# First cross-attention: context loaded first, the first LayerNorm ahead of masks, biases and the values' projection

## The reference, cut to what matters

```python
def _layernorm(x, axis=-1, eps=1e-05):
    m = jnp.mean(x, axis=axis, keepdims=True)
    v = jnp.var(x, axis=axis, keepdims=True)
    return (x - m) / jnp.sqrt(v + eps)

def _L0_xattn_ref(q, k, v, Wq, bq, Wk, bk, Wv, bv, Wo, bo):   # 16 heads of 8
    qh, kh, vh = proj(q, Wq, bq), proj(k, Wk, bk), proj(v, Wv, bv)
    scores = jnp.einsum('bhqd,bhkd->bhqk', qh, kh) / np.sqrt(hd)
    scores = jnp.where(jnp.triu(jnp.ones((S, S), bool)), NEG, scores)
    attn = jax.nn.softmax(scores, axis=-2)
    ...                                            # mixed with vh, then Wo and bo
```

## Time and profile before

| | |
|---|---|
| median of three runs | 3425.03 us |
| the profiled execution's own time | 3413.21 us |
| its span | 3411.4 us |
| TensorE's granted clock, mean | 0.982 of full speed |
| busy, share of the span | PE 95%, DVE 86%, POOL 77%, ACT 70% |
| first matmul of the scores | 20.7 us |
| last step of the first block's pipeline with scores | about 221 us |
| first matmul of the local layers | 244.9 us |

### The profile page before, as it was taken

How to read it: one execution, slowest core, us unless ns; L and a number is a source line. 1 busy time by engine, 2 the same in 40 slices (tenths; PEclk the granted TensorE clock), 3 DMA queues, 4 the chain that set the end, 5 groups by cost and what they waited for, 6 DMA issues and landing times.

```text
span 3411.4 us, 130897 instructions
## 1 busy us (share of the span) xinstructions
PE 3245.9 (95%) x56355; PEld 2054.7 (60%) x56386; DVE 2943.4 (86%) x3343; ACT 2379.1 (70%) x4288; POOL 2639.8 (77%) x1408
## 2 busy tenths in 40 slices
PE   7977999999999999999999999999999999977996
PEld 4545666666666666666666666666666666643554
DVE  6869989889999999998989898898999999935887
ACT  6865677667676767676776776776767676746885
POOL 1229988888888888888888888888888888833576
PEclk9989999999999999999999999999999999988998
DMA  2002333443433344334433334343344333330000
GB/s 94 2 1 64 122 113 111 120 126 114 120 112 112 117 126 119 113 108 126 125 113 117 112 110 123 119 120 113 113 125 125 118 111 112 110 123 1 2 11 17
DMA packets 229188, 336.05 MB, mean 99 GB/s; under 512 B 39046, under 2 KB 151044, under 8 KB 228228
## 3 DMA queue, kind: packets, MB, share of 16 engines
q1 hardware_dynamic: 228612, 327.68, 31.7%
HBM read 124.14 MB, written 102.76 MB: 67 GB/s over the span
## 4 chain that ended last, share of the span: by engine, by line
PE 84%; issue 5%; POOL 4%; ACT 3%; DVE 3%; SPq 0%; DMA 0%; POOLq 0%; DVEq 0%; ACTq 0%
PE psum L732 29%; PE psum L800 10%; PE psum L742 9%; PE psum L786 8%; PE psum L759 8%; PE psum L827 7%; PE psum L838 4%; POOL f_rotated L1154 2%; ACT x_expo L1480 1%; PE psum L817 1%; PE psum L809 1%; ACT x_expo L391 1%; PE psum L1337 1%; PE psum L1347 1%; PE psum L309 1%
## 5 line engine op out<-in xcount | busy, mean ns | idle before, releaser
L732 PE MATMUL psum<-w_qkv,f_xs 128*128 128x512 f32 x2304 | 1081.2, 606 | 18.9 <-issue 14.2
L1154 POOL TENSOR_TENSOR f_rotated<-f_times_cos,f_times_sin 128x1024 f32<-128x1024 f32 x384 | 908.7, 2367 | 9.3 <-DVE f_times_sin L1027 9.3
L1162 POOL TENSOR_TENSOR f_rotated<-f_rotated,f_rnorm 128x1024 f32<-128x1024 f32 x384 | 722.6, 1903 | 38.2 <-ACT f_rnorm L907 11.9
L732 PEld LDWEIGHTS psum<-w_qkv,f_xs 128*128 128x128 f32 x2304 | 410.1, 191 | 402.4 <-issue 393.6
L896 ACT ACTIVATE f_squares<-psum 128x1024 f32<-128x1024 f32 x384 | 392.9, 1023 | 361.4 <-PE psum L732 356.4
L1146 POOL TENSOR_TENSOR f_probs<-f_probs,f_rowsum 128x1024 f32<-128x1024 f32 x192 | 365.2, 1902 | 329.1 <-DVE f_rowsum L1066 329.1
L1026 DVE TENSOR_TENSOR f_times_cos<-psum,rot 128x1024 f32<-128x1024 f32 x384 | 469.8, 1223 | 131.6 <-ACT f_squares L896 127.8
L914 ACT COPY f_qkT<-psum 128x1024 f32<-128x1024 f32 x384 | 369.9, 1013 | 210.8 <-PE psum L742 210.7
L1027 DVE TENSOR_TENSOR f_times_sin<-psum,rot 128x1024 f32<-128x1024 f32 x384 | 466.1, 1214 | 0.0
L1034 DVE TENSOR_REDUCE f_sumsq<-f_squares 128x16 f32<-128x1024 f32 x384 | 463.4, 1209 | 0.0
L742 PEld LDWEIGHTS psum<-consts,f_rotated 128*128 128x128 f32 x3072 | 348.5, 141 | 98.0 <-issue 89.2
(11 more groups left out here) (175 smaller groups left out, 5159.5 us busy)
## 6 DMA issues: line engine op xcount, KB each, us to landing
f_v_moved<-f_v SPq DMA_DIRECT2D x768, 128.0 KB, 2.8
turned_blocks<-w_qkv SPq DMA_DIRECT2D x192, 512.0 KB, 3.0
f_probsT<-turned_blocks SPq DMA_DIRECT2D x768, 128.0 KB, 2.8
w_qkv<-in_l_wqkv SPq DMA_DIRECT2D x18, 512.0 KB, 4.0
w_o<-in_l_wo SPq DMA_DIRECT2D x6, 512.0 KB, 4.6
w_qkv<-in_ctxT SPq DMA_DIRECT2D x1, 2048.0 KB, 8.7
out<-x_f_result SPq DMA_DIRECT2D x8, 256.0 KB, 2.2
w<-in_l_w SPq DMA_DIRECT2D x6, 341.0 KB
```

The costliest lines, as they stand in the source:

```text
L732: mm = pe.matmul(pairs[i][:, j * BANK:(j + 1) * BANK], xs[g % 2][:, u % GB, :], w_qkv[:, part * INNER + j * BANK:part * INNER + (j + 1) * ...
L1154: pool.tensor_tensor(rotated[u % 2][:, part].rearrange("p h (s d) -> p s h d", s=2), halves(times_cos[part][:, :]), halves(times_sin[part] ...
L1162: pool.tensor_tensor(rt, rt, rnorm[u % 2][:, part * H:(part + 1) * H].unsqueeze(2).broadcast_to([P, H, HD]), ALU.mult).then_inc(normalised ...
```

## The change

Four edits. The context's first load is issued ahead of weights and tables; the tables (`consts`) are issued last of these. DVE no longer casts the masks and makes the biases before its first `centre`, but after it, in a function `constants()` called in step -5. ACT waits for the biases in step -3 rather than before its first square. And the lag of `variance_0` goes from -3 to -4, for all eight groups.

```diff
@@ first_attention @@
             MEAN, CENTRE, SQUARE, VARIANCE, ROOT, SCALE = (
-                {"0": -6, "f": 7}, {"0": -6, "f": 7}, {"0": -5, "f": 7}, {"0": -3, "f": 8}, {"0": -3, "f": 8}, {"0": -2, "f": 9})
+                {"0": -6, "f": 7}, {"0": -6, "f": 7}, {"0": -5, "f": 7}, {"0": -4, "f": 8}, {"0": -3, "f": 8}, {"0": -2, "f": 9})
...
             def sp(sp):
-                for dst, src in ((w_k, "wkT"), (b_k, "bk"), (w_v, "wvT"), (w_q, "wqT"), (b_q, "bq"), (w_o, "woT")):
-                    sp.dma_start(dst[:, :], dram[f"x0_{src}"]).then_inc(loaded, 16)
-                sp.dma_start(b_o[:, :], dram["x0_bo"]).then_inc(loaded, 16)
-                sp.dma_start(b_v[:, :], dram["x0_bv"].partition_broadcast(P)).then_inc(loaded, 16)
...
                 sp.dma_start(ctx2[:, first], dram["ctxT"][:, first]).then_inc(ctx_loaded, 16)
+                for dst, src in ((w_v, "wvT"), (w_k, "wkT"), (b_k, "bk"), (w_q, "wqT"), (b_q, "bq"), (w_o, "woT"), (b_o, "bo")):
+                    sp.dma_start(dst[:, :], dram[f"x0_{src}"]).then_inc(loaded, 16)
+                sp.dma_start(b_v[:, :], dram["x0_bv"].partition_broadcast(P)).then_inc(loaded, 16)
+                sp.dma_start(consts[:, :], dram["consts"]).then_inc(consts_loaded, 16)
                 sp.dma_start(x2[:, rest], dram["xT"][:, rest]).then_inc(rest_loaded, 16)
...
             def act(act):
                 act.preload_act_table_set("natural_log_exp_and_others")
-                act.wait_ge(biases_made, BIASES)
                 act.wait_ge(eps_made, 1)
...
                 for step in range(FIRST, LAST):
+                    if step == FIRST + 3:
+                        act.wait_ge(biases_made, BIASES)
...
             def dve(dve):
-                dve.wait_ge(loaded, LOADED)
-                dve.wait_ge(gates_ready, 1)
-                dve.tensor_scalar(b_q[:, :], b_q[:, :], inv_root, None, ALU.mult).then_inc(biases_made, 1)
...
+                def constants():
+                    dve.wait_ge(consts_loaded, 16)
+                    dve.tensor_copy(ident_bf[:, :], ident).then_inc(masks_ready, 1)
...
+                    dve.wait_ge(loaded, LOADED)
+                    dve.wait_ge(gates_ready, 1)
...
                 for step in range(FIRST, LAST):
+                    if step == FIRST + 1:
+                        constants()
```

More of the change, by code:

```diff
@@ L432, in dve @@
             def dve(dve):
-                dve.wait_ge(loaded, LOADED)
-                dve.wait_ge(gates_ready, 1)
-                dve.tensor_scalar(b_q[:, :], b_q[:, :], inv_root, None, ALU.mult).then_inc(biases_made, 1)
-                dve.tensor_scalar(b_k_part[:, :], head_parts, b_k[:, 0:1], None, ALU.mult).then_inc(biases_made, 1)
-                dve.tensor_tensor(gated_b_o[:, :], b_o[:, :], gates[:, 0:1], ALU.mult).then_inc(biases_made, 1)
-                dve.wait_ge(biases_made, BIASES)
+                def constants():
+                    dve.wait_ge(consts_loaded, 16)
+                    dve.tensor_copy(ident_bf[:, :], ident).then_inc(masks_ready, 1)
+                    for g in range(GB):
+                        dve.tensor_copy(mask_past[:, g, :], consts[:, P + NEAR:2 * P + NEAR]).then_inc(masks_ready, 1)
+                    dve.wait_ge(loaded, LOADED)
+                    dve.wait_ge(gates_ready, 1)
+                    dve.tensor_scalar(b_q[:, :], b_q[:, :], inv_root, None, ALU.mult).then_inc(biases_made, 1)
+                    dve.tensor_scalar(b_k_part[:, :], head_parts, b_k[:, 0:1], None, ALU.mult).then_inc(biases_made, 1)
+                    dve.tensor_tensor(gated_b_o[:, :], b_o[:, :], gates[:, 0:1], ALU.mult).then_inc(biases_made, 1)
+                    dve.wait_ge(biases_made, BIASES)
                 dve.wait_ge(x_loaded, 16)
@@ L1777, in _ @@
             sp.dma_start(xres[:, 0:GB * REST, :].rearrange("p b s -> p (b s)"), dram["xT"][:, 0:REST * GT]).then_inc(x_loaded, 16)
-            sp.dma_start(consts[:, :], dram["consts"]).then_inc(consts_loaded, 16)
             sp.dma_start(gates[:, 0:2], dram["g_xattn"].partition_broadcast(P)).then_inc(gates_loaded, 16)
@@ L1803, in _ @@
         def _(dve):
[L1804 to L1807, removed]
             x0_dve(dve)
```

## The result

The changed kernel takes 3443.16 us (median of six runs, 3437.63 to 3452.78), where the kernel before took 3424.65 on the same chip: a ratio of 1.0058, with a 95% interval of 1.0041 to 1.0075, which is 14 to 26 us slower. The forecast was 3445. The profiled execution is the longest of the six (3452.78 us), so its terms may come out larger than the median.

What follows compares the result with a forecast made beforehand. In the first block a DVE-ACT loop sets three steps of four, PE's chain the fourth. Start -2.8, bank wait +18.4 and clock +4.8 give +20.4 us: 3445.4 on a median of 3425.0, range 3437 to 3458.

Steps and rivals of the forecast that it cites:

- The bank wait: Middle of first block, six steps: `mix` gets `variance0`'s bank and waits for the Ln in `root_0`; +18.4 us in sum.
- not won back: Rival, middle: `mix` is late, but the following 6.26 us steps shrink and balance it; within 7 us, 3425; 6%.
- The start: First block's start: earlier context, variance, keys and first scores; -2.8 us, ends -3.5 and +1.
- That load keeps its place in the queue: Start: the values' bias, last of eight small loads, still lands at 9.28, so `project_v` cannot start before 9.3.
- Issued now at 6.40 they land at 10.5: Start: the tables, issued last, take 4.1 us as before, or land at 11.3 with the context's old 4.85.
- Keys are done 2.9 us earlier, at 13.35: Start, PE: with values earlier and the variance no longer between values and keys, keys end at 13.35 instead of 16.24.
- the first scores follow as they did: Start: key biases on DVE and ACT and first scores follow the keys as before; -2.8 us after hand-overs.
- the trace's agreement: Start: the context landed 4.85 us after issue with 2 MB behind it, taken to agree that later loads hold nothing back.
- The clock: Middle, PE: half of the six new gaps halve the clock at 1.6 us each; 4.8 us, range 0 to 18.
- all gaps run cold: Rival, middle: the clock halves at each of six gaps, also through the next scores, 3.3 us each; +35, 3460; 12%.
- 15 to 22: Sign in the changed profile: the local layers, behind the first block, start 15 to 22 us later.
- only the relief is left: Rival, middle: the bank wait is hidden; start gives -2.8, shorter PE chain up to -5.2; 3417; 5%.

Runs made afterwards that it cites:

- the change again: The changed kernel unaltered, run a second time against the kernel before, for a second profile: +26.6 us (20.5 to 32.8).

## Why the prediction was right

*The bank wait: right, in place and size.* `mix` in the six steps got the bank of `variance0` and waits for the Ln behind L398. Moving the turn alone takes the whole loss away, making the bank alone gives it back (+23.9), and the lag alone makes it (+29.0). Forecast were 18.4 us; with the clock held up it is 18.8. The split held as well: 2.62 a step for the bank without the shift (forecast 2.6), and 29.15 - 25.92 = 3.2 with it (3.15).

*It is not hidden and not won back: right.* The three other steps stayed at 6.26 unless the clock fell, and DVE's idle time absorbed nothing.

*The start: -2.8 forecast, a loss of 1.3 and 3.6 us measured* (step 1's `row_sums`, the change again and the change's first profile). The step that failed is "That load keeps its place in the queue, so `project_v` cannot start before 9.3", and beside it "Issued now at 6.40 they land at 10.5": both durations came from rows in which the context's load stood elsewhere. Bias and tables landed 2.2 and 1.8 us later. I had made the tables the danger, and it was the values' bias, which `project_v` waits for. A second step failed with it: "Keys are done 2.9 us earlier, at 13.35", and that "the first scores follow as they did". The keys and the mean behind them ran at the slow rate of the first mean, 1.92 each, and the scores hang on that mean through DVE's centring. Why PE was still slow there is not shown; the windows give a granted clock of 1.00 up to 20 us. And the forecast had no clock term for the start, though the change lengthens PE's gap ahead of the first scores from 1.09 to 2.15 us (2.33 in the second profile). By either alternative in the prediction (-2.8, or +1 through late tables) the result lies nearer the second.

The Trainium skill ("DMA: Bandwidth & Descriptors", queues, rings and completion order) says that each DMA engine consumes the descriptors in ring order. My conclusion from it, that a load is not held back by what is issued behind it, did not hold: with the same loads ahead, 5.6 us with 3 MB behind and 3.4 without. What I had called the trace's agreement was none: behind the context stood 3 MB and not 2, and that row says nothing on what they cost it.

*The clock: 4.8 forecast, 8.2 and 13.2 measured* in the six periods. The price of one fall was about right (1.6; about 1.5 in the kernel with the bank alone). The count was not: I took half of six gaps, since "around the new gaps PE runs without a pause". Each period of the second profile had a fall, and in the first there were seven stretches up to 230 us, the start's among them; three in the middle were 7 to 10 us long and cost more than 1.6 (the period with the 10 us one was 34.9). All six gaps at 1.6 would have been 9.6. What was measured lies between my forecast and the rival "all gaps run cold" (20). The Trainium skill ("TensorE: Matmul & The Clock Gate", Part 1) says that an idle stretch halves the clock. The trace agrees with it in direction: two matmuls in each gap removed all falls ahead of the tail.

*The total was met in part by luck.* The errors of start and clock have the same sign. Beside the profile of before, the parts are 1.3 + 18.8 + 8.2 + 0.6 (behind step 25) = 28.9 us in one profile of the change and 3.6 + 18.8 + 13.2 + 0.6 = 36.2 in the other, where the forecast was 20.4; and the local layers started 28.7 and 36.1 us later, not 15 to 22. The changed kernel took 3443.16 and 3443.59 us in its two comparisons. It is the kernel before that differed: 3424.65 in the first, 3415.35 to 3419.31 in the four others, each on a chip of its own. The forecast stood on 3425.0, so a base some 6 to 10 us high made up for terms that were some 6 us or more short. Of the second comparison's +26.6 (20.5 to 32.8) the forecast +20.4 lies at the very edge.

*The rival "only the relief is left" was wrong twice.* The wait was not hidden, and its 5.2 us would not have been there without the wait. PE runs without a pause from the scores of step 0 (95.05) to the keys behind the mix of step 1 (107.44), so a matmul moved from step 1 to step 0 comes out of and goes into the same chain. I had counted the 0.96 us saved in step 1 without what step 0 adds to the same chain: 0.03 us a period.

What stays open: why the clock fell behind four of the six gaps of 2.55 us and not behind the others, and why one profile of the change had three long stretches and the other none. In the second profile they began near 30.4, 61.1 and 91.8 us; the first of these stands in step 1, where `mix` had waited only 0.86 us, and the distance is that of the gaps themselves. The start's loss to the clock was only read and not tried: no run fills the gap ahead of the first scores. The two kernels with the mended turn, with and without the new start, are not separable within their intervals.

## What to carry to other kernels

Where buffers are dealt in turn, a changed lag re-deals them: after such an edit look for waits that have changed their semaphore, and ask of each when its releaser stands in the same step. Here a matmul moved by one step saved time only where a pause of the engine lay between its old and its new place. A faster start can lengthen the engine's gap ahead of its next work and pay for it in clock. A load's time from issue to landing depended on its neighbours in the queue, those behind it too: when small loads gate the first work, hold back the large ones that nothing needs yet.

## What the runs showed of the hardware

Behind a gap of 2.55 us on PE in dense work the granted clock dropped to 0.50 in four of six places, and with 1.88 us of filler matmuls in a gap of 3.3 it stayed at 1.00 in all six. One fall cost about 1.5 us there, though the two-pass matmul directly behind it took twice as long, since DVE and ACT set the pace again after one or two steps.

In the start, PE stood 1.67 to 2.33 us ahead of the first scores in eight profiles, and in six of them the clock was at 0.50 within 2 us of the scores' start. In the five with 0.69 to 1.44 us it was not.

A 64 KB load, the last of eight small ones, took 3.3 to 3.4 us from issue to landing with either the 512 KB ahead of it moved behind or the 3 MB behind it held back, and 4.9 to 5.7 in the five kernels that had both.
